# A projection in three fp32r products: high and low parts made by ScalarE and GpSimd

## The chip, the cores and the metric

The kernel runs on one core of a Trainium2 chip. The metric is device time in microseconds of one execution; three timed runs of the kernel before gave 1002.29, 999.23 and 1001.32 us, median 1001.32. TensorE (PE) multiplies matrices, VectorE (DVE), ScalarE (ACT) and GpSimd (POOL) do elementwise work, SyncE (SP) issues most transfers. Each engine works through its own list in order and waits on semaphores.

## The reference

One block of a graph network on 3125 nodes with 256 features and 50000 edges: a graph attention layer, a mixing layer in hyperbolic space and a layer of eight experts, each added to the rows. The change concerns the first product of the graph attention alone:

```python
xn = _layernorm(x, axis=-1)
h_prime = (xn @ W + b).reshape(n, 8, 32)
h_src = jnp.sum(h_prime * a_src, axis=2)      # per node and head
h_trg = jnp.sum(h_prime * a_trg, axis=2)
```

The attention weights per edge come from h_src[src] + h_trg[trg] through leaky_relu and exp, and the rows h_prime[src] are summed per target with these weights. The later parts use h_prime only through these sums.

## The kernel before

**Tiles.** The 3125 nodes are 25 tiles of 128 (NT = 25). The features are two chunks of 128 (KC = 2). `FM` (traced as feat_rows) holds x transposed, features on partitions; it is loaded from a transposed copy of x in three parts of 8, 8 and 9 tiles (ROW_PARTS, semaphores xt_part). `x_in` holds x with nodes on partitions, in the same three parts, for the row statistics.

**Weights.** TensorE turns the centred W into bank `b_hte` (line 822) and multiplies it with the attention vectors into `b_z` (lines 827 and 829). ScalarE copies both into `wx`, 256 + 16 = 272 columns (HW) for each chunk, and the bias row into `hbias` (lines 538 to 541, semaphore wx_ready, 3 in the end).

**Projection.** `project(t)` on TensorE (line 839) multiplies tile t of FM, as the stationary operand, with `wx` in plain f32, two matmuls of 272 columns in the program (four records in the trace, bank<-oh,feat_rows, line 847), into one of eight banks (AHEAD = 8): it waits until the bank's tile eight before has been read (hst_done). VectorE's `project(t)` (line 1265) scales the first 264 columns with the row's inverse deviation, adds the bias row and writes ACC (traced as sums; semaphore hp_ready). ScalarE's `targets_part(t)` (line 547) waits for hp_ready, takes the last 16 columns into `hst` (line 549) and signals hst_done. SP stores each row tile of ACC to the table projected_rows (line 403).

**Order around it.** VectorE's list: statistics of part 0 (`part_stats`, lines 1212 to 1221), `part_roots(0)`, then the 25 tiles, with part_stats(1) and (2) after tiles 3 and 10 and part_roots(1) and (2) after tiles 5 and 12; then the norms of the rows (from line 1231). ScalarE's list: `inverse_root` for part 0, then targets_part for the 25 tiles, with inverse_root for parts 1 and 2 after tiles 3 and 10 (lines 553 and 554); each waits for the statistics of that part. TensorE warms up with transposes (line 815) before. GpSimd makes constants, waits for the target numbers, casts them to 16 bits (`d16`, line 508), and then starts the edge gathers (line 503), which wait for all 25 stores of projected rows. SP sends d16 out before the store of tile TARGETS_IN (20).

**Behind the projection** TensorE turns the normalised rows (line 836) and forms their covariance (line 879), 33 groups of edges are gathered, weighted and summed (lines 1389, 1443, 923), beside the mixing layer; then the experts follow in two layers and an output, which are already done as three fp32r products of high and low parts (lines 1051 to 1053).

Of the kernel before, what the change touches and what calls it, by code (L numbers as in the profile page):

```python
# [9 lines left out]
F32 = mybir.dt.float32  # L10
# [46 lines left out]
CUT = 18  # L57
LEAD = 2
AHEAD = 8
ROW_PARTS = [(0, 8), (8, 16), (16, NT)]  # L60
TURNED = 8
WARM = 24
# [1 line left out]
LEADING = 2  # L64
STATS_AT = {3: 1, 10: 2}
ROOTS_AT = {5: 1, 12: 2}
TARGETS_IN = 20
PARTS = 3
XS = 4

# [67 lines left out]
def program(nc, a, out):  # L138
    with ExitStack() as ctx:
# [48 lines left out]
            x_all = early_sb("x_in", NT * XP)  # L188
        x_in = x_all[:, :].rearrange("p (t f) -> p t f", f=XP)


        FM = sb("feat_rows", [P, KC, NPAD])
        mixed = FM[:, :, :].rearrange("p c (t n) -> p t c n", n=P)
# [87 lines left out]
        xst = [uflat[:, i * XS * F:(i + 1) * XS * F].rearrange("p (t f) -> p t f", f=F) for i in range(2)]  # L281
        d16 = ohT[1][:, :].bitcast(I16)[0:NG, 0:EG]
        ohf = [oh[i][:, :, :].rearrange("p c w -> p (c w)") for i in range(2)]
        wx = ohf[0][:, 0:KC * HW].rearrange("p (k n) -> p k n", k=KC)
        hbias = ohf[0][:, KC * HW:(KC + 1) * HW]
        wT = ohf[1][:, 0:KC * F].rearrange("p (c n) -> p c n", c=KC)
        bcolb = ohf[1][:, KC * F:KC * F + 256].rearrange("p (c m) -> p c m", c=KC)
# [15 lines left out]
        for names_ in (  # L303
            "x_pad x_last xt_pad wa_in w_in b_in w_mix w_ffn edge_fill edges idn ablk_zero consts",
            "vchain achain gchain rsq_in rsq_out",
            "wt_ready wt_mm wa_ready wa_mm wx_ready hst_done rng_ready rng_mm dst_in d16_ready d16_out",
            "rows_in xs_ready sym_tr tr_done fs_ready proj_mm hp_ready tout",
            "cm_in cm_tr cm_red cm_mm exs_in exs_out k_mm shifted cov_mm s_copied",
            "sw_mm prod_ready var_mm baff_ready acc_init",
            "z_mm z_evac u_mm u_evac fsq_ready qk_ready eps_ready",  # L310
            "o_ready o_tr oT_ready r_mm mixed_ready no2_ready",
            "dstb_free win_tmp win_ready hte_ready z_part z_done zl_ready exp_done msg_ready",
            "seg_ready acc_done g_free xoT xhte xoh xseg",
            "ft_ready nf2_ready th_in th_out m_ready faff_in faff_out wr_hi wr_lo",
            "mx_tr mx_red mx_mm winv_ready weighed rstd_in rstd_out xs2_in xs2_ready tr2_done",
            "frh_ready frl_ready lg_mm sm_in sm_out gates g3_hi g3_in gt_tr gt_ready bo_clear bo_in bo_mm x2b ff_ready scaled rows_added",
            "w_hi w_lo h1_mm h1_r h1_hi h1_lo h2_mm h2_r h2_hi h2_lo y_mm y_add y_tile out_done out_act",
        ):
            s.update({k: sem(k) for k in names_.split()})
# [152 lines left out]
        @block.gpsimd  # L472
        def _(pool):
            g = nc.gpsimd
            chain = Chain(pool, s["gchain"])
            g.memset(x_in[:, NT - 1, 0:F], 0.0).then_inc(s["x_pad"], 1)
            g.memset(FM[:, :, N:NPAD], 0.0).then_inc(s["xt_pad"], 1)
            g.memset(ablk[:, :, :], 0.0).then_inc(s["ablk_zero"], 1)
            g.memset(ones[:, :], 1.0).then_inc(s["consts"], 1)
            chain.link(g.memset(ident[:, :], 0.0))  # L480
            g.affine_select(out=ident[:, :], in_=ident[:, :], compare_op=ALU.not_equal, fill=1.0, base=0,
                            pattern=[[-1, P]], channel_multiplier=1).then_inc(s["idn"], 1)
            g.memset(src_l[:, NG - 1, :], 0).then_inc(s["edge_fill"], 1)
            g.memset(dst_l[:, NG - 1, :], PAD_DST).then_inc(s["edge_fill"], 1)
            g.memset(ip[:, 1:MC + 1, :], 0.0).then_inc(s["consts"], 1)
            g.iota(row_i, pattern=[[1, P]], base=0, channel_multiplier=0).then_inc(s["consts"], 1)
            g.iota(col_i[:, :], pattern=[[0, 1]], base=0, channel_multiplier=1).then_inc(s["consts"], 1)
            g.memset(avg[:, :], 1.0 / P).then_inc(s["consts"], 1)
            g.memset(x_in[:, :, F:XP], 1.0).then_inc(s["consts"], 1)

            def gather(grp):
                slot, t, paced, settled = grp % SLOTS, grp - LEAD - MIX0, grp >= SLOTS, grp >= 2 * SLOTS
                need(pool, s["g_free"], grp - SLOTS + 1)
                if paced:
                    need(pool, s["msg_ready"], grp - LEAD)
                elif grp == 3:
                    pool.wait_ge(s["cov_mm"], 1)
                for c in range(CHUNKS[grp]):
                    if settled and c == 5:
                        need(pool, s["hte_ready"], grp - LEAD + 2)  # L500
                    if settled and c == 9 and t < NT:
                        pool.wait_ge(s["u_mm"], 3 * t + 3)
                    g.indirect_dma_start(  # L503
                        out=G[slot][:, c, :], out_offset=None, in_=table[:, :],
                        in_offset=bass.IndirectOffsetOnAxis(ap=src_l[:, grp, c:c + 1], axis=0),
                    ).then_inc(gath[slot], 16)
            pool.wait_ge(s["dst_in"], 48)
            g.tensor_copy(d16, dst_rows).then_inc(s["d16_ready"], 1)
            pool.wait_ge(s["edges"], 16 * 6)
            pool.wait_ge(s["tout"], 16 * NT)  # L510
            for grp in range(NG):
                gather(grp)

            pool.wait_ge(s["r_mm"], NT)
            g.memset(bo_raw, 0.0).then_inc(s["bo_clear"], 1)
# [3 lines left out]
        def _(act):  # L519
# [15 lines left out]
                    ins = A.copy(ablk[rows, c, h:h + H + 1:H], acol[rows, c:c + 3:2])  # L535
            ins.then_inc(s["wa_ready"], 1)
            act.wait_ge(s["wt_mm"], 1)
            A.copy(wx[:, :, 0:F], b_hte[:, :].rearrange("p (k f) -> p k f", k=KC)).then_inc(s["wx_ready"], 1)
            act.wait_ge(s["wa_mm"], 1)
            A.copy(wx[:, :, F:HW], b_z[:, 0:KC * 2 * H].rearrange("p (k h) -> p k h", k=KC)).then_inc(s["wx_ready"], 1)  # L540
            A.copy(hbias[:, F:HW], b_z[:, 64:64 + 2 * H]).then_inc(s["wx_ready"], 1)

            def turned(t):
# [13 lines left out]
                A.activation(x_in[:, t, 0:F], x_in[:, t, 0:F], ACT.Identity, bias=nd["nb"][:, t:t + 1], scale=nd["scale"][:, t:t + 1]).then_inc(s["xs_ready"], 1)  # L557

            inverse_root(nd["rstd"], nd["t1"], 1, slice(*ROW_PARTS[0]))
            for t in range(NT):  # L560
                targets_part(t)
                if t in STATS_AT:
                    inverse_root(nd["rstd"], nd["t1"], STATS_AT[t] + 1, slice(*ROW_PARTS[STATS_AT[t]]))
# [246 lines left out]
        def _(pe):  # L810
# [26 lines left out]
                ins.then_inc(s["tr_done"], 1)  # L837

            def project(t):
                for i, (lo, hi) in enumerate(ROW_PARTS):  # L840
                    if t == lo:
                        pe.wait_ge(xt_part[i], 16)
                if t == NT - 1:
                    pe.wait_ge(s["xt_pad"], 1)
                need(pe, s["hst_done"], t - AHEAD + 1)
                for c in range(KC):
                    ins = T.matmul(project_bank(t)[:, 0:HW], FM[:, c, t * P:(t + 1) * P], wx[:, c, :], start=(c == 0), stop=(c == KC - 1))  # L847
                ins.then_inc(s["proj_mm"], 1)

            keep_busy(WARM_TOO)  # L850
            pe.wait_ge(s["wx_ready"], 3)
            for t in range(NT):
                project(t)

# [316 lines left out]
        def _(dve):  # L1171
# [109 lines left out]
                                rng_f[:, :, None].broadcast_to([NG, 4, NG]), ALU.mult).then_inc(s["rng_ready"], 1)  # L1281

            part_stats(0)
            part_roots(0)
            dve.wait_ge(s["wx_ready"], 3)
            dve.wait_ge(s["b_in"], 16)
# [598 lines left out]
```

## Time and profile before

| | |
|---|---|
| timed runs | 1002.29, 999.23, 1001.32 us |
| profiled execution | 999.06 us, span 997.0 us |
| busy, share of the span | PE 907.3 us (91%), DVE 751.3 (75%), ACT 582.0 (58%), POOL 378.2 (38%) |
| projection on TensorE | 12.10 to 36.14 us, 100 recorded matmuls |
| its accumulations on VectorE | 14.27 to 36.67 us, 25 |
| first edge gather | 39.76 us |

Times in the trace count from the span's start. A busy share is an average over all stages; the stage of the change is the first 40 us, and what it is bound by is read from the rows below. The chain of waits goes back from the last instruction to what released it. PEclk is the granted clock of TensorE, 1.00 being 2.4 GHz and 0.50 being 1.2 GHz.

### The profile page before, as it was taken

To read this page: it belongs to the slowest core of one execution; us is meant where nothing else is said; L and a number is where in the kernel's file an instruction comes from. 1 tells how busy PE (TensorE), PEld (TensorE's weight loads), DVE (VectorE), ACT (ScalarE), POOL (GpSimd) and SP (SyncE) were. 2 spreads that over 40 slices of the span, in tenths; PEclk is the share of its full clock that TensorE was granted. 3 is DMA by queue.
4 is the path that set the end of the run, shared out by engine and by line. 5 is a ranking of instruction groups with operands and counts; after the bars stand their busy time and mean duration, and the time that the engine had idled before them with its cause. 6 is when DMAs were issued, how large, how long until landed. Compare 5 with 4: busy or idle time off the path is not lost.

```text
span 997.0 us, 14575 instructions
## 1 busy us (share of the span) xinstructions
PE 907.3 (91%) x4968; PEld 786.9 (79%) x4968; DVE 751.3 (75%) x1465; ACT 582.0 (58%) x1210; POOL 378.2 (38%) x410
## 2 busy tenths in 40 slices
PE   8698799999989988887654899999999999999997
PEld 7487688888877877776543788998989888888886
DVE  6978788887767668777787788876565777777877
ACT  2370366666655666565144657767566666676764
POOL 1377777777777777777772000000000000000000
PEclk9888899999999999999777899999999999999999
DMA  9844545445545545545663012001010000000013
GB/s 309 265 107 134 146 140 140 133 134 141 142 125 139 140 125 141 142 126 140 175 183 93 1 33 77 1 1 33 1 33 1 27 6 15 19 1 1 1 42 87
DMA packets 51176, 92.18 MB, mean 92 GB/s; under 512 B 9780, under 2 KB 33384, under 8 KB 51083
## 3 DMA queue, kind: packets, MB, share of 16 engines
q0 software_dynamic: 18768, 52.88, 19.7%
q1 hardware_dynamic: 31596, 37.86, 12.1%
q8 instruction: 50, 0.82, 0.3%
q10 hardware_dynamic: 719, 0.27, 0.1%
q14 instruction: 43, 0.35, 0.1%
HBM read 84.30 MB, written 6.68 MB: 91 GB/s over the span
## 4 chain that ended last, share of the span: by engine, by line
PE 50%; POOL 23%; issue 10%; DVE 10%; ACT 5%; DMA 1%; DVEq 0%; POOLq 0%; ACTq 0%
POOL G L503 23%; PE bank L1051 9%; PE bank L1053 9%; PE bank L1052 9%; PE bank L923 4%; PE bank L1117 3%; PE bank L1120 3%; PE bank L847 2%; PE bank L958 2%; PE bank L879 2%; PE bank L1118 1%; PE bank L1119 1%; PE bank L969 1%; ACT hid L748 1%; DVE G L1443 1%
## 5 line engine op out<-in xcount | busy, mean ns | idle before, releaser
L503 POOL DMA_INDIRECT G<-projected_rows,src_l x391 | 373.8, 956 | 131.7 <-issue 117.3
L748 ACT ACTIVATE hid<-bank,faff 128x512 f32<-128x512 f32 (+2 forms) x224 | 157.1, 722 | 104.1 <-PE bank L1053 102.2
L923 PE MATMUL bank<-G,oh 128*128 128x264 f32 x782 | 188.3, 399 | 20.3 <-DVE G L1443 20.1
L923 PEld LDWEIGHTS bank<-G,oh 128*128 128x128 f32 x782 | 153.4, 197 | 48.6 <-DVE G L1443 21.3
L1443 DVE TENSOR_TENSOR G<-G,bank 128x3072 f32<-128x3072 f32 (+1 forms) x33 | 109.1, 3306 | 0.0
L958 PE MATMUL bank<-feat_rows,wqkv 128*128 128x256 f32 (+1 forms) x312 | 77.5, 395 | 19.2 <-ACT TT L624 8.1
L1741 DVE TENSOR_TENSOR hil<-hid,hil 128x1024 fp32r<-128x1024 f32 (+2 forms) x56 | 60.8, 1085 | 40.6 <-ACT hil L758 40.4
L958 PEld LDWEIGHTS bank<-feat_rows,wqkv 128*128 128x128 f32 x312 | 60.6, 202 | 30.7 <-ACT TT L624 10.2
L1051 PE MATMUL bank<-frh,ew 128*128 128x512 f32 (+3 forms) x228 | 84.0, 368 | 0.8 <-ACT hid L748 0.7
L1053 PE MATMUL bank<-frh,ew 128*128 128x512 f32 (+3 forms) x228 | 82.4, 362 | 0.0
L1052 PE MATMUL bank<-frl,ew 128*128 128x512 f32 (+3 forms) x228 | 82.4, 361 | 0.0
L1051 PE MATMUL bank<-hil,ew 128*128 128x512 f32 (+2 forms) x224 | 81.6, 364 | 0.0
L1053 PE MATMUL bank<-hil,ew 128*128 128x512 f32 (+2 forms) x224 | 81.2, 362 | 0.0
L1052 PE MATMUL bank<-hil,ew 128*128 128x512 f32 (+2 forms) x224 | 81.1, 362 | 0.0
L587 ACT ACTIVATE G<-zed,negc 128x96 f32<-128x96 f32 (+1 forms) x33 | 12.5, 379 | 98.7 <-DVE zed L1416 98.7
L1389 DVE TENSOR_REDUCE zed<-bank 128x96 f32<-128x288 f32 (+1 forms) x33 | 14.9, 451 | 61.5 <-DMA G<-projected_rows,src_l 57.8
L1761 DVE SCALAR_TENSOR_TENSOR feat_rows<-bank,gate,feat_rows 128x256 f32<-128x256 f32 (+1 forms) x117 | 56.6, 484 | 4.1
L1420 DVE TENSOR_TENSOR oh<-key,bank 128x1536 f32<-128x1536 f32 (+1 forms) x33 | 56.9, 1724 | 2.0 <-ACT bank L591 2.0
L1760 DVE SCALAR_TENSOR_TENSOR feat_rows<-bank,gate,feat_rows 128x256 f32<-128x256 f32 (+1 forms) x117 | 55.6, 475 | 0.0
L758 ACT CAST hil<-hid 128x1024 fp32r<-128x1024 f32 (+2 forms) x56 | 52.7, 942 | 4.4
L1741 DVE TENSOR_TENSOR even<-hid,even 128x1024 fp32r<-128x1024 f32 (+2 forms) x28 | 30.5, 1089 | 32.3 <-ACT even L758 32.3
L1741 DVE TENSOR_TENSOR odd<-hid,odd 128x1024 fp32r<-128x1024 f32 (+2 forms) x28 | 30.4, 1087 | 26.9 <-ACT odd L758 26.9
(345 smaller groups left out, 2021.6 us busy)
## 6 DMA issues: line engine op xcount, KB each, us to landing
dstb<-targets SPq DMA_DIRECT2D x32, 384.0 KB, 3.8
G<-projected_rows,src_l POOLq DMA_INDIRECT x391
projected_rows<-sums SPq DMA_DIRECT2D x25, 132.0 KB, 2.2
x_in<-in_x SPq DMA_DIRECT2D x3, 1024.0 KB, 11.5
out<-feat_rows SPq DMA_DIRECT2D x23, 128.0 KB, 2.2
feat_rows<-in_xT SPq DMA_DIRECT2D x2, 1024.0 KB, 11.3
U<-in_x SPq DMA_DIRECT2D x4, 512.0 KB, 6.6
TT<-in_W SPq DMA_DIRECT2D x8, 256.0 KB, 3.2
```

The source lines that it names most:

```text
L503: g.indirect_dma_start(out=G[slot][:, c, :], out_offset=None, in_=table[:, :], in_offset=bass.IndirectOffsetOnAxis(ap=src_l[:, grp, c:c + ...
L748: A.activation(hid[layer][:, m, 0:cols], bank[2 * layer + m][:, 0:cols], ACT.Relu, bias=faff[:, 2 * layer + 1, j:j + 1], scale=faff[:, 2 * ...
L923: ins = T.matmul(b_seg[g % 2][:, 0:ROW], oh[g % 2][:, c, :], G[g % SLOTS][:, c, :], start=(c == 0), stop=(c == ch - 1))
L958: ins = T.matmul(b_z[:, i * 256:i * 256 + cols], wqkv[:, k, c * P:(c + 1) * P], FM[:, k, start:start + cols], start=(k == 0), stop=(k == K ...
L1051: T.matmul(out_, lh, rh, start=(k == 0), stop=False)
L1052: T.matmul(out_, lh, rl, start=False, stop=False)
L1053: return T.matmul(out_, ll, rh, start=False, stop=(k == KC - 1))
L1420: return V.tensor_tensor(out_, keys[:, :, None].broadcast_to([P, ch, P]), b_seg[par][:, ROWC:ROWC + P][:, None, :].broadcast_to([P, ch, P] ...
L1443: V.tensor_tensor(m3, m3, exps(par, ch)[:, :, :, None].broadcast_to([P, ch, H, DH]), ALU.mult).then_inc(s["msg_ready"], 1)
L1741: V.tensor_tensor(hidl[layer][par][:, :, 0:cols], hid[layer][:, :, 0:cols], hidh[layer][par][:, :, 0:cols].bitcast(F32), ALU.subtract).the ...
L1760: link(V.scalar_tensor_tensor(out=m, in0=high, scalar=gate[0:rows, t, e:e + 1], in1=m, op0=ALU.mult, op1=ALU.add))
L1761: ins = V.scalar_tensor_tensor(out=m, in0=low_, scalar=gate[0:rows, t, e:e + 1], in1=m, op0=ALU.mult, op1=ALU.add)
```

## The change

The product x W is split in three: with x = xh + xl and W = Wh + Wl, where xh and Wh are the values rounded to fp32r, it adds xh Wh, xh Wl and xl Wh, for both chunks, so six fp32r matmuls of 272 columns per tile. ScalarE rounds the tiles of FM into a ring of 12 tiles (`xh`), eight ahead of targets_part in its list, tile 0 still before the weights are complete and tiles 1 to 7 after inverse_root of part 0. GpSimd subtracts (`xl = FM - xh`) into a second ring, tile after tile, and casts the targets after tile 21 (TARGETS_IN is 22 now). VectorE makes the low part of the weights in two subtractions, between part_stats(0) and part_roots(0). TensorE waits for wx_low, and per tile for xh and xl in place of the loads. The rings lie where the edge gathers' buffers G0 to G2 are later. Left out below are the line of semaphore names and the removed `wx`.

```diff
+RING = 12
+SPLIT_AHEAD = 8
-TARGETS_IN = 20
+TARGETS_IN = 22
...
+            x_split = [ring_sb(f"x_split{i}", RING * F) for i in range(2)]
+            w_split = [ring_sb(f"w_split{i}", KC * HW) for i in range(2)]
...
-            pool.wait_ge(s["dst_in"], 48)
-            g.tensor_copy(d16, dst_rows).then_inc(s["d16_ready"], 1)
+            pool.wait_ge(s["xt_pad"], 1)
+            for t in range(NT):
+                pool.wait_ge(s["xh_ready"], t + 1)
+                need(pool, s["proj_mm"], t - RING + 1)
+                g.tensor_tensor(xl[:, t % RING], FM[:, :, t * P:(t + 1) * P], xh[:, t % RING].bitcast(F32), ALU.subtract).then_inc(s["xl_ready"], 1)
+                if t == TARGETS_IN - 1:
+                    pool.wait_ge(s["dst_in"], 48)
+                    g.tensor_copy(d16, dst_rows).then_inc(s["d16_ready"], 1)
...
+            def high_rows(t):
+                for i, (lo, hi) in enumerate(ROW_PARTS):
+                    if t == lo:
+                        act.wait_ge(xt_part[i], 16)
+                if t == NT - 1:
+                    act.wait_ge(s["xt_pad"], 1)
+                need(act, s["proj_mm"], t - RING + 1)
+                A.copy(xh[:, t % RING], FM[:, :, t * P:(t + 1) * P]).then_inc(s["xh_ready"], 1)
+
+            high_rows(0)
             act.wait_ge(s["wa_mm"], 1)
...
             inverse_root(nd["rstd"], nd["t1"], 1, slice(*ROW_PARTS[0]))
+            for t in range(1, SPLIT_AHEAD):
+                high_rows(t)
             for t in range(NT):
+                if t + SPLIT_AHEAD < NT:
+                    high_rows(t + SPLIT_AHEAD)
                 targets_part(t)
...
             def project(t):
-                for i, (lo, hi) in enumerate(ROW_PARTS):
-                    if t == lo:
-                        pe.wait_ge(xt_part[i], 16)
-                if t == NT - 1:
-                    pe.wait_ge(s["xt_pad"], 1)
+                pe.wait_ge(s["xh_ready"], t + 1)
+                pe.wait_ge(s["xl_ready"], t + 1)
                 need(pe, s["hst_done"], t - AHEAD + 1)
+                o = project_bank(t)[:, 0:HW]
                 for c in range(KC):
-                    ins = T.matmul(project_bank(t)[:, 0:HW], FM[:, c, t * P:(t + 1) * P], wx[:, c, :], start=(c == 0), stop=(c == KC - 1))
+                    T.matmul(o, xh[:, t % RING, c], wxh[:, c, :], start=(c == 0), stop=False)
+                    T.matmul(o, xh[:, t % RING, c], wxl[:, c, :], start=False, stop=False)
+                    ins = T.matmul(o, xl[:, t % RING, c], wxh[:, c, :], start=False, stop=(c == KC - 1))
                 ins.then_inc(s["proj_mm"], 1)
 
             keep_busy(WARM_TOO)
             pe.wait_ge(s["wx_ready"], 3)
+            pe.wait_ge(s["wx_low"], 2)
...
             part_stats(0)
+            dve.wait_ge(s["wx_ready"], 1)
+            V.tensor_tensor(wxl[:, :, 0:F], b_hte[:, :].rearrange("p (k f) -> p k f", k=KC), wxh[:, :, 0:F].bitcast(F32), ALU.subtract).then_inc(s["wx_low"], 1)
+            dve.wait_ge(s["wx_ready"], 3)
+            V.tensor_tensor(wxl[:, :, F:HW], b_z[:, 0:KC * 2 * H].rearrange("p (k h) -> p k h", k=KC), wxh[:, :, F:HW].bitcast(F32), ALU.subtract).then_inc(s["wx_low"], 1)
             part_roots(0)
```

## Rows read from the trace of the kernel before

**Rows 1.** Chain of waits, 10 to 50 us: start, us, what.
```profile
12.31 23.85 PE bank L847 x100
```

**Rows 2.** Waits, 0 to 48 us: total us, times, longest.
```profile
POOL G L503 <- DMA projected_rows<-sums: 12.9, 1, 12.9
...
DVE sums L1267 <- PE bank L847: 2.0, 5, 0.4
```

**Rows 3.** Timeline of VectorE, 12 to 38 us: start, us, instruction, [idle before].
```profile
12.66 0.17 DVE L1221 TENSOR_SCALAR nodes<-mv 128x8 f32<-128x8 f32 x1
...
15.10 0.49 DVE L1267 SCALAR_TENSOR_TENSOR sums<-bank,nodes,oh 128x264 f32<-128x264 f32 x1 [0.33 <-PE bank L847]
...
16.93 0.49 DVE L1267 SCALAR_TENSOR_TENSOR sums<-bank,nodes,oh 128x264 f32<-128x264 f32 x1 [0.42 <-PE bank L847]
...
24.98 3.02 DVE L1210 BATCH_NORM_STATS2 stats<-x_in 128x6 f32<-128x256 f32 x9
...
28.98 0.17 DVE L1221 TENSOR_SCALAR nodes<-mv 128x9 f32<-128x9 f32 x1
...
30.67 4.17 DVE L1267 SCALAR_TENSOR_TENSOR sums<-bank,nodes,oh 128x264 f32<-128x264 f32 x10
35.26 0.49 DVE L1267 SCALAR_TENSOR_TENSOR sums<-bank,nodes,oh 128x264 f32<-128x264 f32 x1 [0.42 <-PE bank L847]
36.18 0.49 DVE L1267 SCALAR_TENSOR_TENSOR sums<-bank,nodes,oh 128x264 f32<-128x264 f32 x1 [0.42 <-PE bank L847]
```

**Rows 4.** Timeline of TensorE in the expert layers, 699 to 712 us.
```profile
701.66 0.28 PE L1051 MATMUL bank<-ew,odd 128*128 128x256 f32 x1
...
704.41 0.28 PE L1053 MATMUL bank<-ew,odd 128*128 128x256 f32 x1
...
705.33 0.34 PE L1052 MATMUL bank<-frl,ew 128*128 128x384 f32 x1
...
707.06 0.33 PE L1053 MATMUL bank<-frh,ew 128*128 128x384 f32 x1
```

**Rows 5.** Timeline of TensorE, 7 to 12.5 us: the second warm-up block.
```profile
10.26 2.05 PE L815 MATMUL bank<-ip 128*128 128x128 f32 x10
```

**Rows 6.** Stretches: us, busy of PE, PEld, DVE, ACT, POOL, PEclk, DMA share, GB/s.
```profile
10.50:11.00 0.50, 0.50 (x5) 0.50 (x4) 0.50 (x3) 0.21 (x2) 0.00 (x0) 0.62 1.09 387
...
14.00:14.50 0.50, 0.50 (x4) 0.42 (x3) 0.36 (x2) 0.00 (x0) 0.00 (x0) 0.97 1.03 410
...
41.00:41.50 0.50, 0.00 (x0) 0.00 (x0) 0.43 (x3) 0.00 (x0) 0.30 (x1) 0.84 1.06 399
...
58.00:58.50 0.50, 0.50 (x4) 0.45 (x3) 0.50 (x3) 0.19 (x1) 0.50 (x1) 0.59 0.88 211
```

**Rows 7.** VectorE's instructions by line and shape: count, busy us, mean ns, idle before.
```profile
L1716 DVE TENSOR_TENSOR frl<-bank,frh 128x512 fp32r<-128x512 f32 x11 | 7.5, 691 | 6.8 <-ACT frh L730 6.8
```

**Rows 8.** Instructions that write feat_rows, 0 to 48 us: the loads, issue to landing.
```profile
L383 SPq DMA_DIRECT2D feat_rows<-in_xT x3: 592/3485/3692, 1.7 to 11.5; - x3
...
DMA to landing us min/median/max: 9.1/13.0/13.6
```

**Rows 9.** ScalarE's instructions by line and shape.
```profile
L635 ACT ACTIVATE exr<-feat_rows 128x256 bf16<-128x256 f32 x25 | 10.4, 416 | 6.8 <-DVE feat_rows L1567 5.3
...
L549 ACT ACTIVATE hst<-bank,nodes 128x16 f32<-128x16 f32 x25 | 6.8, 273 | 8.7 <-DVE sums L1267 7.0
...
L730 ACT CAST frh<-bank 128x256 fp32r<-128x256 f32 x3 | 1.1, 376 | 0.0
```

**Rows 10.** Timeline of ScalarE, 29 to 37.5 us: inverse_root of the third part.
```profile
29.19 0.21 ACT L553 ACTIVATE nodes<-nodes 128x9 f32<-128x9 f32 x1 [3.82 <-DVE nodes L1221]
```

**Rows 11.** GpSimd's instructions by line and shape.
```profile
L503 POOL DMA_INDIRECT G<-projected_rows,src_l x391 | 373.8, 956 | 131.7 <-issue 117.3 <-DMA projected_rows<-sums 12.9 <-DVE G L1443 0.6
L508 POOL CAST ohT<-U 33x1536 int16<-33x1536 int32 x1 | 1.5, 1456 | 22.0 <-DMA U<-in_dst 22.0
...
L476 POOL MEMSET x_in<- 128x256 f32 x1 | 0.3, 311 | 0.3 <-POOLq L1878 0.3
```

More of the change, by code:

```diff
@@ L189, in program, with ring_sb @@
         x_in = x_all[:, :].rearrange("p (t f) -> p t f", f=XP)
+        with ExitStack() as ring_stack:
+            def ring_sb(name, columns_, dt=F32R):
+                return ring_stack.enter_context(nc.sbuf_tensor(name, [P, columns_], dt))
+            ring_sb("ring_under_rows", KC * NPAD, F32)
+            ring_sb("ring_under_sums", (NT + 1) * ROW, F32)
+            x_split = [ring_sb(f"x_split{i}", RING * F) for i in range(2)]
+            w_split = [ring_sb(f"w_split{i}", KC * HW) for i in range(2)]
+        xh, xl = (b[:, :].rearrange("p (t k n) -> p t k n", t=RING, k=KC) for b in x_split)
+        wxh, wxl = (b[:, :].rearrange("p (k n) -> p k n", k=KC) for b in w_split)
         FM = sb("feat_rows", [P, KC, NPAD])
@@ L283, in program @@
         ohf = [oh[i][:, :, :].rearrange("p c w -> p (c w)") for i in range(2)]
-        wx = ohf[0][:, 0:KC * HW].rearrange("p (k n) -> p k n", k=KC)
         hbias = ohf[0][:, KC * HW:(KC + 1) * HW]
@@ L305, in program @@
             "vchain achain gchain rsq_in rsq_out",
-            "wt_ready wt_mm wa_ready wa_mm wx_ready hst_done rng_ready rng_mm dst_in d16_ready d16_out",
+            "wt_ready wt_mm wa_ready wa_mm wx_ready wx_low xh_ready xl_ready hst_done rng_ready rng_mm dst_in d16_ready d16_out",
             "rows_in xs_ready sym_tr tr_done fs_ready proj_mm hp_ready tout",
@@ L537, in _ @@
             act.wait_ge(s["wt_mm"], 1)
-            A.copy(wx[:, :, 0:F], b_hte[:, :].rearrange("p (k f) -> p k f", k=KC)).then_inc(s["wx_ready"], 1)
+            A.copy(wxh[:, :, 0:F], b_hte[:, :].rearrange("p (k f) -> p k f", k=KC)).then_inc(s["wx_ready"], 1)
+            def high_rows(t):
[7 more added lines that the diff above has]
+            high_rows(0)
             act.wait_ge(s["wa_mm"], 1)
-            A.copy(wx[:, :, F:HW], b_z[:, 0:KC * 2 * H].rearrange("p (k h) -> p k h", k=KC)).then_inc(s["wx_ready"], 1)
+            A.copy(wxh[:, :, F:HW], b_z[:, 0:KC * 2 * H].rearrange("p (k h) -> p k h", k=KC)).then_inc(s["wx_ready"], 1)
             A.copy(hbias[:, F:HW], b_z[:, 64:64 + 2 * H]).then_inc(s["wx_ready"], 1)
```

## The prediction

> **What bounds the kernel now.** I read the chain of waits first. It runs straight through the projection: 23.85 us of matmuls of line 847 from 12.31 us on [rows 1], then VectorE's last accumulation of line 1267, then the small node arithmetic and the turning of the rows. So what counts is when the last accumulation ends: 36.18 + 0.49 = 36.67 us [rows 3]. The second thing that starts there is GpSimd's gather, which waits until all 25 tiles of projected rows are stored [rows 2]; it moves with the same end. I therefore carry a shift of this end one to one to the end of the kernel.
>
> The chain names TensorE, but the wait view corrects it: in the whole projection VectorE waits for line 847 only 2.0 us, in five pieces [rows 2]. The order of VectorE's work shows why [rows 3]. It waits a little in tiles 1 to 3, falls behind while it takes the second and the third part of the row statistics (3.02 us of BATCH_NORM_STATS2 for the third, plus small steps), and then catches up: ten accumulations in 4.17 us, 0.42 us each, back to back from 30.67 us. Only tiles 23 and 24 wait for TensorE again, 0.42 us each. So TensorE and VectorE are level at the end, and a faster TensorE alone can win no more than about those two waits, and only if nothing else comes late.
>
> **TensorE's own work.** Before: four recorded matmuls of a tile; the last two accumulations start 0.92 us apart [rows 3], so about 0.23 us per pass. After: six single-precision-round (fp32r) matmuls with 272 columns. The expert layers have such products: 24 with 256 columns start 701.66 to 704.41, that is 0.120 us each, and 11 with 384 columns start 705.33 to 707.06, 0.173 us each [rows 4]. For 272 columns I interpolate 0.127 us, so 0.76 us per tile, 19.0 us for 25 tiles against some 23: about 4 us less TensorE work, if its clock is high.
>
> **The start.** TensorE's warm-up ends at 12.31 [rows 5], and the first product followed at once. Now it waits for wx_low, the low part of the weights. VectorE makes that after part_stats(0), which signals at about 12.8 (12.66 + 0.17, [rows 3]), in two subtractions. The nearest row of the large one (PSUM minus SBUF into fp32r, 128x512) is 691 ns [rows 7]; the small one (32 columns) is bounded by the 0.17 us of the tiny steps. End: about 13.7. ScalarE meanwhile waits for the first third of the transposed rows, which is there no sooner than 1.7 + 9.1 = 10.8 us [rows 8], and rounds tile 0; GpSimd's subtraction of tile 0 ends about 12; neither is late. So TensorE starts at 13.75, not at 12.1, and is idle for some 1.4 us.
>
> That gap touches the clock. The granted clock fell to half (1.2 GHz) at about 10.6 and was full again (2.4 GHz) from 14.0 [rows 6], with TensorE busy without a gap from the second warm-up block on [rows 5]. With a gap in that stretch I don't expect the return at 14.0. At 1.2 GHz a tile costs 6 x 272 / 1.2 GHz = 1.36 us. Only the first four tiles count here, because VectorE waits for TensorE only up to tile 3. If the clock is high at once, tile 3 is streamed at 13.75 + 4 x 0.76 = 16.8; if all four run low, at 19.2. I take 18.4, nearer to the low clock, because after the next long gap the clock stayed low from 41.4 to 58.4, long after TensorE had work again [rows 6]. VectorE starts about 0.25 us behind a tile's stream (before, tile 1 was streamed at 14.85, two tiles from 12.1 at 0.92 per tile and twice that before 14.0, and accumulated from 15.10), so its accumulation of tile 3 starts at 18.65, where it was 16.93 [rows 3]: 1.7 us late; by the two ends 0.1 or 2.5 us late.
>
> From there to tile 22 VectorE's list is the same and nearly without waits, and TensorE is ahead of it, so the 1.7 us are carried: the third part's statistics signal at 30.85 (before about 29.15, 28.98 + 0.17) and the burst may begin at 32.4.
>
> **The end.** Here the new queues decide. ScalarE has 25 more copies of 128x256 from SBUF. The nearest rows are 376 ns (cast from PSUM) and 416 ns (square from SBUF) [rows 9]; I take 0.41, with 0.27 for the head column (line 549) 0.65 us per tile as they overlap a little. Spread over 23 us this hides behind VectorE. But high_rows(19) stands behind inverse_root(2) in ScalarE's order, and that waits for the third part's statistics: before, 29.19 [rows 10], now about 30.9, done 31.35. So tiles 19 to 24 are rounded at 31.8, 32.4, 33.05, 33.7, 34.3, 35.0, and TensorE, which could have finished tile 18 by about 30, waits for them. VectorE is covered by the finished banks for that time.
>
> GpSimd's 25 subtractions are not in the trace (two inputs, 128x256). From below: a memset of 256 columns, 311 ns. From above: the longest GpSimd row, 956 ns. Between: the cast with one input took 1456 ns for 1536 elements, 0.95 ns each [rows 11]; with 0.1 us fixed, one reading of 256 is 0.34 and two readings 0.59. I take 0.65 with its two waits. The GPSIMD Engine Reference of the Trainium skill (section 3.1) gives 4497 ns for a two-input add of 2048 fp32 elements; an estimate from that page is 0.6 us for 256, and the sum would stay as it is; no run so far shows it.
>
> Tiles 19 to 21 leave GpSimd at 32.45, 33.1, 33.75. Then the cast of the targets, 1.46 us [rows 11], stands in the same queue, at tile 21: it was hidden at 25.4 before, now it stands before tiles 22 to 24, and no product of theirs may start without it. They come at 35.85, 36.5, 37.15. TensorE needs 0.76 us each: tile 24 is streamed at 38.2, VectorE accumulates it from 38.4 to 38.9. Against 36.67 that is **2.2 us later**. Without the cast in the way it would be 37.8; with VectorE alone as the bound 37.4. The cast's result itself (SP's store at tile 22) delays nothing, as the stores of tiles 22 to 24 come later anyway.
>
> **Sum.** The profiled execution took 999.06 us (span 997.0, 2.1 around it). 999.06 + 2.2 = 1001.3. The three timed runs have the median 1001.32, and the mean of all four is 1000.5, so the profiled one was a quick one; I put the forecast at 1000.5 + 2.2 = **1002.7**. The 4 us of TensorE work buy nothing, since VectorE was level with it.
>
> **Rivals.**
> Rival A, VectorE alone bounds: the clock returns as early as before, and the rounding and the subtraction of the last tiles arrive in time, so that the waits of tiles 23 and 24 (0.84 us) and 0.4 us of their TensorE tail vanish: 1.2 us faster, 999.3. For it: VectorE's 0.42 us per tile is a firm row. Against it: the order behind inverse_root(2) and the cast at tile 21.
> Rival B, GpSimd becomes the bound. It decides from 0.76 us per subtraction on, TensorE's own pace. At 0.956, its upper bound, tile t leaves it at about 13.8 + 0.96 t: tile 21 at 34.9 with tile 22 queued, the cast to 36.4, tile 24 at 39.3, accumulated at 40.8: 4.1 us slower, 1004.6. For it: 25 two-input operations that no row shows. The SBUF page of the Trainium skill ("Who interferes with whom") says that a VectorE instruction with two SBUF inputs and a GpSimd instruction that reads SBUF shut each other out; VectorE's long operations here have at most one, so I give that no time of its own.
> Rival C, a second drop of the clock: TensorE waits up to 2.5 us at tile 19, and the last six tiles run at 1.36 instead of 0.76 us, 3.6 us more: 5.8 us slower, 1006.3. Against it: TensorE did almost nothing from 36.1 on, and the clock fell only at 41.4 [rows 6].
> Rival D, the products don't run at the rate of the expert layers (272 columns lie between measured 256 and 384, so I doubt it); at 0.23 us each a tile costs 1.38 us, and 25 of them last from 13.75 to 48.3, 12 us longer than before: 1012.5.
>
> **Chances.** Forecast (0 to 3 us slower) 0.62; A 0.15; B 0.13; C 0.07; D 0.03. What a measurement of this kernel can tell from no change is 0.3%, 3.0 us. Faster by more would need a gain that VectorE's list has no room for, 0.06; slower by more is B, C, D and the upper part of the forecast, 0.24; the same 0.70. The range runs from A to C, 999.2 to 1006.3; the forecast's own is 1000.5 to 1003.8.
>
> **What would show it.** The first product at about 13.7 and the clock still low at 14.0 and back before 19; products 0.127 us apart; VectorE's accumulation of tile 3 at 18.6; ScalarE's copies at 0.41, GpSimd's subtractions near 0.6 to 0.65 us; TensorE waiting for the subtraction at tile 19 and at tile 22 behind the cast; the last accumulation ending at about 38.9. The prediction is wrong if that end lies before 36.5, or if the end shifts and the total doesn't follow it.

## The result, and the profile after

The changed kernel took 1004.12 us in the median of six runs (1002.91 to 1004.54) against 999.22 us for six runs of the kernel before (998.47 to 1002.29): a ratio of 1.0037 with a 95% interval of [1.0027, 1.0047], which is 3.7 us slower. (The two medians lie 4.9 us apart, since the six runs of before scatter over 3.8 us.) The profiled execution took 1004.07 us with a span of 1002.2 us, 5.0 us more than the profiled one of before. The forecast was 2.2 us slower. The direction and most of the steps came as written, and one step on the path failed: VectorE's list did not stay as long as it was.

Waits of the changed kernel, 0 to 48 us (total us, times, longest), to hold against [rows 2]:

```profile
POOL x_split L522 <- ACT x_split L564: 16.1, 5, 8.0
...
DVE sums L1300 <- PE bank L879: 2.0, 5, 0.8
...
PE bank L877 <- POOL x_split L522: 2.6, 1, 2.6
...
PE bank L877 <- DVE w_split L1320: 1.8, 1, 1.8
```

TensorE has two new waits, one for the low weights and one for GpSimd's subtraction. VectorE waits for TensorE 2.0 us in five pieces, as much as before, so its own list still fills the rest of the stage, and that list has grown. Its timeline in the changed kernel, to hold against [rows 3] (L1300 is the accumulation, L1243 the row statistics, L1209 to L1212 the four small Newton steps of `part_roots`):

```profile
11.46 0.70 DVE L1218 TENSOR_TENSOR mv<-stats 128x8 f32<-128x8 f32 x1
12.09 0.16 DVE L1219 TENSOR_TENSOR mv<-stats 128x8 f32<-128x8 f32 x1
...
18.53 0.49 DVE L1300 SCALAR_TENSOR_TENSOR sums<-bank,nodes,oh 128x264 f32<-128x264 f32 x1 [0.26 <-PE bank L879]
18.94 2.70 DVE L1243 BATCH_NORM_STATS2 stats<-x_in 128x6 f32<-128x256 f32 x8
...
23.48 0.15 DVE L1209 TENSOR_TENSOR nodes<-nodes 128x8 f32<-128x8 f32 x1
23.67 0.72 DVE L1210 TENSOR_TENSOR nodes<-nodes 128x8 f32<-128x8 f32 x1
24.42 0.66 DVE L1211 TENSOR_SCALAR nodes<-nodes 128x8 f32<-128x8 f32 x1
25.11 0.67 DVE L1212 TENSOR_TENSOR nodes<-nodes 128x8 f32<-128x8 f32 x1
25.82 2.09 DVE L1300 SCALAR_TENSOR_TENSOR sums<-bank,nodes,oh 128x264 f32<-128x264 f32 x5
27.82 3.03 DVE L1243 BATCH_NORM_STATS2 stats<-x_in 128x6 f32<-128x256 f32 x9
...
32.71 0.16 DVE L1209 TENSOR_TENSOR nodes<-nodes 128x9 f32<-128x9 f32 x1
32.90 0.70 DVE L1210 TENSOR_TENSOR nodes<-nodes 128x9 f32<-128x9 f32 x1
33.64 0.66 DVE L1211 TENSOR_SCALAR nodes<-nodes 128x9 f32<-128x9 f32 x1
34.34 0.65 DVE L1212 TENSOR_TENSOR nodes<-nodes 128x9 f32<-128x9 f32 x1
35.02 4.72 DVE L1300 SCALAR_TENSOR_TENSOR sums<-bank,nodes,oh 128x264 f32<-128x264 f32 x11
40.00 0.49 DVE L1300 SCALAR_TENSOR_TENSOR sums<-bank,nodes,oh 128x264 f32<-128x264 f32 x1 [0.25 <-PE bank L879]
```

The same steps in the kernel before (L1176 to L1179 there), on the same timeline of VectorE:

```profile
21.89 0.16 DVE L1176 TENSOR_TENSOR nodes<-nodes 128x8 f32<-128x8 f32 x1
...
22.97 2.09 DVE L1267 SCALAR_TENSOR_TENSOR sums<-bank,nodes,oh 128x264 f32<-128x264 f32 x5 [0.31 <-DVE nodes L1179]
...
29.86 0.16 DVE L1176 TENSOR_TENSOR nodes<-nodes 128x9 f32<-128x9 f32 x1
30.05 0.17 DVE L1177 TENSOR_TENSOR nodes<-nodes 128x9 f32<-128x9 f32 x1
30.26 0.17 DVE L1178 TENSOR_SCALAR nodes<-nodes 128x9 f32<-128x9 f32 x1
30.47 0.17 DVE L1179 TENSOR_TENSOR nodes<-nodes 128x9 f32<-128x9 f32 x1
```

Steps over eight or nine columns that took 0.17 us take 0.65 to 0.72 us. The third part's group of four lasts from 32.71 to 35.02, 2.31 us, where it lasted from 29.86 to 30.67, 0.81 us. The second part's lasts 2.34 us (23.48 to 25.82); in the trace before it ran from 21.89 to 22.97, 1.08 us, 0.31 of it a wait. GpSimd's timeline in the changed kernel says what else goes on at those times:

```profile
11.40 0.73 POOL L522 TENSOR_TENSOR x_split<-feat_rows,x_split 128x256 fp32r<-128x256 f32 x1 [8.05 <-ACT x_split L564]
13.86 7.67 POOL L522 TENSOR_TENSOR x_split<-feat_rows,x_split 128x256 fp32r<-128x256 f32 x11 [1.73 <-ACT x_split L564]
23.63 2.13 POOL L522 TENSOR_TENSOR x_split<-feat_rows,x_split 128x256 fp32r<-128x256 f32 x3 [2.09 <-ACT x_split L564]
26.99 2.83 POOL L522 TENSOR_TENSOR x_split<-feat_rows,x_split 128x256 fp32r<-128x256 f32 x4 [1.23 <-ACT x_split L564]
32.86 2.10 POOL L522 TENSOR_TENSOR x_split<-feat_rows,x_split 128x256 fp32r<-128x256 f32 x3 [3.04 <-ACT x_split L564]
34.91 1.45 POOL L525 CAST ohT<-U 33x1536 int16<-33x1536 int32 x1
```

Every long small step lies inside a run of subtractions (11.46 in the first, 23.67 to 25.11 in the third, 32.90 to 34.34 in the fifth; two Newton steps of the first part, at 14.01 and 14.66, took 0.62 and 0.65 us in the second), and every short one outside, or begun just before a run starts (23.48, 32.71) or as it ends (12.09). The long Newton steps of the second and third part start 0.75, 0.69 and 0.74, 0.70 us apart, which is the pace of the subtractions (7.67 us for eleven, 0.70 each): here VectorE gets one small step in for each subtraction. L1210 and L1212 read two tensors in SBUF; L1211, a TENSOR_SCALAR, reads only one and is as long (0.66), so two inputs are not the whole condition.

The order of the kernel makes them meet. ScalarE's `inverse_root` releases two things at once: the Newton steps on VectorE, and, because the roundings queue behind it, the next three roundings and with them three subtractions.

The end of the projection is then a sum of four pieces. The accumulation of tile 3 starts 1.6 us later (18.53 against 16.93 [rows 3]); the second group costs 2.34 - 1.08 = 1.26 us more and the third 2.31 - 0.81 = 1.50; and the two waits for TensorE at the end (0.84 us [rows 3]) have become one of 0.25; short waits inside the merged rows and rounding make up the 0.05 that is left. That is +3.8: the last accumulation ends at 40.49 instead of 36.67.

Stretches of the changed kernel (columns as in [rows 6]; PEclk is third from the end):

```profile
16.00:17.00 1.00, 1.00 (x6) 1.00 (x6) 0.24 (x2) 0.59 (x3) 1.00 (x2) 0.50 1.09 351
17.00:18.00 1.00, 1.00 (x10) 1.00 (x9) 0.61 (x2) 0.85 (x3) 1.00 (x2) 0.99 1.10 352
30.00:33.00 3.00, 1.07 (x9) 0.84 (x7) 2.83 (x15) 0.94 (x5) 0.14 (x1) 1.00 0.02 7
33.00:34.00 1.00, 0.32 (x2) 0.35 (x3) 0.96 (x2) 0.71 (x3) 1.00 (x2) 1.00 0.64 221
34.00:35.00 1.00, 1.00 (x7) 1.00 (x6) 0.95 (x2) 0.00 (x0) 1.00 (x3) 0.54 0.14 50
35.00:37.00 2.00, 2.00 (x11) 2.00 (x10) 1.98 (x5) 1.45 (x7) 2.00 (x2) 0.50 0.25 87
```

The clock is low (0.50, 1.2 GHz) until 17.0 and comes back with TensorE busy. It falls a second time at 34.0, after TensorE had stood for 2.62 us, until 33.69, behind `inverse_root(2)`. There VectorE is mostly the later of the two: it is busy 1.98 of the 2.00 us from 35 to 37.

### The profile page after: what moved, and what is told of

It is laid out like the page before. It is cut to its first block, busy times and chain, and to the rows that moved or that the text cites. A ratio compares the mean times of both kernels' runs of the same rounds, so it can differ in the third digit from the quotient of the medians.

```text
span 1002.2 us, 14765 instructions
## 1 busy us (share of the span) xinstructions
PE 906.0 (90%) x5018; PEld 788.9 (79%) x5018; DVE 756.2 (75%) x1467; ACT 588.2 (59%) x1235; POOL 395.9 (40%) x435
## 4 chain that ended last, share of the span: by engine, by line
PE 47%; POOL 27%; issue 11%; DVE 9%; ACT 4%; DMA 1%; POOLq 0%; DVEq 0%; ACTq 0%
POOL G L514 26%; PE bank L1084 10%; PE bank L1086 9%; PE bank L1085 9%; PE bank L956 3%; PE bank L1150 2%; PE bank L1153 2%; PE bank L912 2%; PE bank L991 2%; PE bank L1151 1%; PE bank L1152 1%; POOL x_split L522 1%; ACT hid L780 1%; PE bank L1002 1%; PE bank L868 1%
```

## The experiments

The theory was that VectorE's small steps wait for GpSimd's subtractions (the lock theory). The rivals were that the late start after the low weights, or the clock that is low in it, makes the loss; that TensorE, starved at tile 19, does; and that the total follows something after the projection. The runs were made in three jobs, each on one chip with its own runs of the kernel before: e1, e2, e3, e5 beside a median of 1001.64 us (23 runs, 998.93 to 1004.48), e4, e6, e7, e8 beside 999.86 us (27), c1, c2 beside 1000.58 us (20). The kernel before thus moves by 1.8 us between the jobs, so totals of different jobs are compared by their ratios, and the totals expected in microseconds only loosely. "End" is the end of the last accumulation.

**e1: no subtraction.** The third product takes the high rows again, so the term of low rows times high weights is left out of the result; the cast of the targets runs first on GpSimd.

```diff
-                g.tensor_tensor(xl[:, t % RING], ..., ALU.subtract).then_inc(s["xl_ready"], 1)
...
-                pe.wait_ge(s["xl_ready"], t + 1)
...
-                    ins = T.matmul(o, xl[:, t % RING, c], wxh[:, c, :], ...)
+                    ins = T.matmul(o, xh[:, t % RING, c], wxh[:, c, :], ...)
```

> The changed kernel without GpSimd's subtraction: the third product of each tile takes the high part xh in place of xl (so xl Wh is left out of the result), TensorE has as many matmuls as before, and GpSimd casts the targets as early as in the kernel before. Theory (lock): GpSimd's subtractions shut out VectorE's small two-input Newton steps in part_roots(1) and (2), 2.3 us each instead of 0.8 to 1.1. Without them the steps are back at 0.17 us and the last accumulation ends at 40.49 - 1.25 - 1.5 = 37.7 us, give or take 0.4; total about 1001.3. Rival (starved TensorE): the loss is made by TensorE's wait of 2.6 us behind inverse_root(2) and the second drop of its clock, and the Newton steps are only long in passing; this order on ScalarE is left as it is, so the last accumulation stays at 39.5 us or later and the total at 1003 or more.

Median 1001.35 us, ratio 0.9994 [0.9983, 1.0006]. All Newton steps are back at 0.16 to 0.17 us, although ScalarE still rounds beside them, so its roundings are not what makes them long. The end, 38.98, lies between the two theories, 1.3 us later than mine: tile 3 came 0.6 us later than in the changed kernel (19.12), and without the long steps VectorE arrives earlier and now meets TensorE, whose clock was at 0.50 from 33 to 36 us after a similar pause (four waits of 0.20 to 0.41 us). The total equals the median of before in this job, but not because the end does, which is 2.3 us later than 36.67: the profiled execution, 1001.20, is 2.1 us above the profiled one of before (999.06). That the total came out as expected is in part luck.

**e2: the kernel before, with 29 idle subtractions.** GpSimd subtracts rows into a buffer that nobody reads yet; besides, the cast of the targets stands among the subtractions, and two later waits make sure that they are done.

```diff
+            for t in range(29):
+                rows = FM[:, :, t % 8 * P:(t % 8 + 1) * P]
+                g.tensor_tensor(G[t // EC][:, t % EC, 0:F]..., rows, rows, ALU.subtract).then_inc(s["extra"], 1)
...
```

> The kernel before with 29 subtractions of 128x256 on GpSimd alone, from the landing of the first third of the transposed rows on, back to back until about 33 us, their results unused; nothing else of the change. Theory (lock): the small steps of VectorE with two inputs from SBUF take up to 0.7 us each in the statistics and in the Newton steps, wherever a subtraction runs; the last accumulation ends 2 to 7 us later than 36.67 and the total rises by as much, to 1001 to 1006; the matmuls stay as they are. Rival (starved TensorE): TensorE's list and ScalarE's are those of before, so the end stays within 0.5 us of 36.67 and the total within 1 us of 999.2.

Median 1007.99 us (1003.74 to 1010.8), ratio 1.0066 [1.0042, 1.0089]. VectorE's timeline, with the Newton steps of the first and of the second part:

```profile
15.43 0.62 DVE L1183 TENSOR_TENSOR nodes<-nodes 128x8 f32<-128x8 f32 x1 [0.52 <-ACT nodes L560]
16.08 0.54 DVE L1184 TENSOR_TENSOR nodes<-nodes 128x8 f32<-128x8 f32 x1
...
19.40 2.70 DVE L1217 BATCH_NORM_STATS2 stats<-x_in 128x6 f32<-128x256 f32 x8
...
24.95 0.16 DVE L1183 TENSOR_TENSOR nodes<-nodes 128x8 f32<-128x8 f32 x1
25.14 0.17 DVE L1184 TENSOR_TENSOR nodes<-nodes 128x8 f32<-128x8 f32 x1
```

GpSimd's timeline of the same run:

```profile
10.82 12.62 POOL L510 TENSOR_TENSOR G<-feat_rows 128x256 f32<-128x256 f32 x22 [7.47 <-DMA feat_rows<-in_xT]
...
27.02 4.03 POOL L510 TENSOR_TENSOR G<-feat_rows 128x256 f32<-128x256 f32 x7
```

With no other part of the change, the same steps are long inside the run of subtractions and short after it (of fifteen small steps that began in that run, three slipped through at 0.16 to 0.19 us). The statistics proper are not slowed: eight in 2.70 us inside the run, 0.34 each, like the nine in 3.02 of [rows 3]. Nor are the accumulations. So it is the small steps and GpSimd's subtraction, whatever TensorE computes. The end was 39.4, 2.7 us late, as expected. The total was not: the runs spread over 7 us, their median lies above the 1006 that I had allowed, and the profiled execution (1003.74) is the fastest of the six. Where the rest of this kernel's loss arises stays open.

**e3: low weights earlier**, inside the statistics of the first part.

```diff
+                    if t == 3:
+                        dve.wait_ge(s["wx_ready"], 1)
+                        V.tensor_tensor(wxl[:, :, 0:F], ..., ALU.subtract).then_inc(s["wx_low"], 1)
...
```

> The changed kernel with VectorE's two subtractions for the low weights moved into the first part's statistics (the large one after four of the eight BATCH_NORM_STATS2, the small one after the eighth). Theory (the start costs 1.6 us by TensorE's gap and the clock that stays low): the first product follows the warm-up at about 12.2, the clock is back at about 14, VectorE's accumulation of tile 3 starts at 16.3 to 17.0 instead of 18.53, and the end comes 1.5 to 2 us earlier, total about 1002.3. Rival (the loss comes only from the lock and the end, and the start is made up by VectorE's slack later): the end stays within 0.4 us of 40.49 and the total at 1004.

Median 1004.54 us, ratio 1.0025 [1.0013, 1.0038]. The first product came at 12.23 and the clock stayed high (1.00 from 12 to 19 us), yet tile 3 was accumulated only at 17.43: tile 1 now waited for its subtraction (GpSimd's second run still begins at 14.03). Of the 1.1 us gained there only 0.4 are left at the end (40.11): the statistics' small steps moved into that GpSimd run and took 0.48 and 0.78 us. This is what the rival had said (an end within 0.4 us of 40.49): an earlier start is worth little while the lock moves along. That the edit kept the clock high is not shown: in other executions it fell at other times (at 10.2 in the changed kernel, 12.4 in e1).

**e4: seven more warm-up transposes.**

```diff
-WARM_TOO = 10
+WARM_TOO = 17
```

> The changed kernel with 17 in place of 10 transposes in the second warm-up block, so that TensorE has work until the low weights are there and its clock comes back earlier. Theory (lock): the accumulation of tile 3 comes about 1 to 1.5 us earlier, but then the statistics of part 1 end while GpSimd's first run of subtractions still goes on (it ended at 21.5 us), their small steps get long in turn, and the end of the projection gains 0.5 us at most: total 1003.5 to 1004.2. Rival (the start's 1.6 us are lost for good by the clock and come back with it): the end is 1 us or more earlier, total 1003 or less.

Median 1003.77 us, ratio 1.0033 [1.002, 1.0046]. TensorE had no pause, but at 0.50 the 17 transposes lasted from 10.86 to 14.73, so the first product came at 14.37 instead of 13.80, and the clock returned only between 16 and 17 us (0.82). Tile 3 came at 18.55, so nothing was gained, where both theories had expected at least 1 us. The clock was already at 0.50 from 10 us on in this execution. Since the start did not move, the run does not test what it was made for, and what the gap and the low clock cost at the start stays untested.

**e5: eleven tiles ahead instead of eight.**

```diff
-SPLIT_AHEAD = 8
+SPLIT_AHEAD = 11
```

> The changed kernel with ScalarE rounding eleven tiles ahead in place of eight (SPLIT_AHEAD 11), so that TensorE has rounded tiles up to 21 before inverse_root(2). Theory (lock): TensorE's wait of 2.6 us and the second drop of the clock go away, but they are covered by VectorE's catching up; as long as a subtraction runs beside part_roots the end moves by no more than 0.5 us, total 1003.5 to 1004.2; if the subtractions move out of part_roots the Newton steps get short and the end comes up to 2.7 us earlier, and the two go together. Rival (starved TensorE): the end comes 2 us or more earlier although the Newton steps stay long.

Median 1006.65 us, ratio 1.0047 [1.0032, 1.0061], slower still. The longer GpSimd run (fourteen subtractions, 13.99 to 23.76) now covers the second part's statistics. VectorE's timeline has the longest small step of all runs:

```profile
22.10 1.70 DVE L1217 TENSOR_TENSOR nodes<-stats 128x8 f32<-128x8 f32 x1
```

It began inside that run and ended with it (23.80), after more than two subtractions. TensorE's clock fell again (0.50 from 35 to 38 us), but the last twelve accumulations ran without a wait for it and ended at 42.08, so starvation of TensorE is not what sets the end here. The lock theory had allowed 0.5 us, and missed: I had not looked where the longer run would end.

**e6: Newton operands in PSUM**, for the second and third part; everything is computed.

```diff
+        def moved(v, i):
+            at = 0 if v is nd["t1"] else 64
+            return bank[7][:, at:at + NT] if i else v
...
-AHEAD = 8
+AHEAD = 7
...
```

> The changed kernel with the variance and the temporary of the Newton steps of parts 1 and 2 in a PSUM bank kept free for it (seven banks for the projection in place of eight), so that none of the four steps has two inputs from SBUF; GpSimd's subtractions stay where they are. Theory (lock, through VectorE's second way into SBUF): the four steps take 0.2 us each although subtractions run beside them, part_roots(1) and (2) last 0.8 to 1.0 us in place of 2.3; the end moves forward by 1.2 to 1.6 us only, because TensorE, late behind inverse_root(2) and at the low clock, is the next bound; total about 1002.5. Rival (VectorE is slowed by anything GpSimd does, not by the port): the steps stay at 0.6 us or more and the total does not fall.

Median 1002.06 us, ratio 1.002 [1.0011, 1.0029]; end 38.87, 1.6 us sooner. GpSimd's timeline of this run:

```profile
13.94 7.68 POOL L527 TENSOR_TENSOR x_split<-feat_rows,x_split 128x256 fp32r<-128x256 f32 x11 [1.82 <-ACT x_split L569]
...
31.10 2.13 POOL L527 TENSOR_TENSOR x_split<-feat_rows,x_split 128x256 fp32r<-128x256 f32 x3 [2.77 <-ACT x_split L569]
```

VectorE's timeline, with the last two Newton steps of the first part, whose operands stay in SBUF, and the four of the third:

```profile
14.08 0.61 DVE L1267 TENSOR_SCALAR nodes<-nodes 128x8 f32<-128x8 f32 x1
14.73 0.65 DVE L1268 TENSOR_TENSOR nodes<-nodes 128x8 f32<-128x8 f32 x1
...
30.98 0.16 DVE L1265 TENSOR_TENSOR bank<-nodes,bank 128x9 f32<-128x9 f32 x1
31.18 0.18 DVE L1266 TENSOR_TENSOR bank<-bank,nodes 128x9 f32<-128x9 f32 x1
31.39 0.17 DVE L1267 TENSOR_SCALAR bank<-bank 128x9 f32<-128x9 f32 x1
31.59 0.17 DVE L1268 TENSOR_TENSOR nodes<-nodes,bank 128x9 f32<-128x9 f32 x1
```

The same lines (L1267, L1268) take 0.61 and 0.65 us beside subtractions with their operands in SBUF, and 0.17 us beside subtractions with the variance and the temporary in PSUM: the multiplications then read one operand in SBUF, the TENSOR_SCALAR none. (The first multiplications come in another order, and the projection has seven banks.) That is the lock, switched off by the place of the operands. The two groups last 0.81 and 0.82 us, 3.0 us less than in the changed kernel, and tile 3 came 0.7 us sooner (17.85); of these 3.7 us, 1.6 reach the end: TensorE, at 0.50 from 33 to 35 us, is now what VectorE waits for (0.81 us and three times 0.26), and a step of the second part's statistics, at 21.00, took 0.65 us beside a subtraction.

**e7: e1, and tiles 19 to 21 rounded before `inverse_root(2)`** (the same term is left out).

```diff
...
+                if t == 10:
+                    for tt in range(19, 22):
+                        high_rows(tt)
...
```

> As e1 (no subtraction on GpSimd, third product with xh in place of xl), and in addition ScalarE rounds tiles 19 to 21 ahead of inverse_root(2), so that TensorE is not left without work before the last tiles. In e1 the last four accumulations waited 1.1 us for TensorE, whose clock had dropped. Theory (lock first, starved TensorE second): these waits go, the end comes 0.7 to 1.1 us earlier than in e1 (38.98), total 1000.3 to 1001. Rival (TensorE's wait costs nothing, VectorE's list alone sets the end): no change against e1, within 0.3 us.

Median 1000.57 us, ratio 1.0005 [0.9996, 1.0014]. The clock stays at 1.00 from 29 to 39 us, the last twelve accumulations run without a wait, and the end is 36.39. VectorE's timeline:

```profile
31.50 4.89 DVE L1296 SCALAR_TENSOR_TENSOR sums<-bank,nodes,oh 128x264 f32<-128x264 f32 x12
```

That is 2.6 us before e1's end, more than expected, partly because tile 3 was 1.1 us earlier than in e1 here. So without lock and starvation the end is where it was before (36.67), and VectorE's list bounds. The faster products do buy something: these twelve took 6.00 us before (30.67 to 36.67), 1.1 us more, about the 1.2 us of rival A. But the later start takes as much away (tile 3 at 18.02, before 16.93).

**e8: the full product with all of it mended** (low weights early, tiles 1 to 3 and 18 to 20 rounded ahead of their `inverse_root`, Newton in PSUM, the cast after tile 14).

```diff
-SPLIT_AHEAD = 8
+SPLIT_AHEAD = 7
...
-TARGETS_IN = 22
+TARGETS_IN = 15
...
+                if t == 10:
+                    for tt in range(18, 21):
+                        high_rows(tt)
...
```

> The full product with what the runs point to: low weights made within the first statistics (as e3), tiles 1 to 3 rounded before inverse_root(0), rounding seven ahead, tiles 18 to 20 rounded before inverse_root(2), Newton steps of parts 1 and 2 through PSUM (as e6, seven banks), the cast of the targets after tile 14. Theory: tile 3 is accumulated by about 17, the Newton steps are short, only the small steps of the statistics can still meet a subtraction (0.5 to 1.5 us); the end at 36 to 37.3 and the total within 1 us of the kernel before. Rival (something else of the change costs, such as the banks or the transfers): the total stays above that of the kernel before by 2 us or more.

Median 1002.86 us, ratio 1.0023 [1.0014, 1.0033]; end 40.97, a miss by over 3 us. The total stays 3.0 us above before, as the rival had said, but not by banks or transfers. The Newton steps of the second and third part are short. The subtractions moved forward met the small steps that still lie in SBUF: those of the first part, two of its statistics (0.70 and 0.66 us) and two Newton steps (0.70 and 0.65), so that tile 3 came at 18.6 and not by 17, and those of the third part's statistics. VectorE's timeline there:

```profile
29.40 0.58 DVE L1227 TENSOR_TENSOR nodes<-stats 128x9 f32<-128x9 f32 x1
29.91 0.77 DVE L1228 TENSOR_TENSOR mv<-stats 128x9 f32<-128x9 f32 x1
30.60 0.76 DVE L1229 TENSOR_TENSOR mv<-stats 128x9 f32<-128x9 f32 x1
31.39 0.64 DVE L1230 TENSOR_TENSOR nodes<-nodes 128x9 f32<-128x9 f32 x1
```

GpSimd's run there lasts from 27.82 to 32.00. The delayed `inverse_root(2)` starved TensorE again, and the last five tiles waited for it.

**c1 and c2: the changed kernel unedited, and e6 again, on one chip.**

> The changed kernel unedited, beside the next one on one chip, so that the two can be compared in timed runs and not only in one profile each. If the shift in the projection is a steady one, the ratio to the kernel before lies again between 1.0027 and 1.0047 and the last accumulation ends within 0.4 us of 40.5. If it came from one lucky or unlucky phase of the clock, the ratio falls below 1.002.

> The kernel with the Newton operands of the second and third part in PSUM, on the same chip as the changed kernel. Lock theory: 1.2 to 2.2 us below the changed kernel's median, as the last accumulation ends 1.6 us sooner. Rival, that the end of the projection doesn't reach the total and only the clock's phase further on decides: within 0.7 us of the changed kernel.

c1: median 1004.08 us, ratio 1.0037 [1.0025, 1.0049], as in the first six runs. Its end was 41.29, outside my 0.4 us, because the clock came back only between 19 and 20 us there. It did not fall a second time in this execution (1.00 from 34 to 40 us), and the loss was the same, so that drop is not its cause. VectorE's last twelve accumulations:

```profile
36.15 5.14 DVE L1300 SCALAR_TENSOR_TENSOR sums<-bank,nodes,oh 128x264 f32<-128x264 f32 x12
```

c2: median 1001.40 us, ratio 1.0009 [0.9996, 1.0022]: 2.7 us below c1, above the 1.2 to 2.2 that I had allowed, with an end of 39.01. Part of the difference in the ends is c1's later clock (tile 3 at 19.65 against 18.51). Still, moving two small operands out of GpSimd's way takes back 2.7 of the 3.5 us that c1's median lies above before, in timed runs. No kernel here is faster than the one before beyond its interval.

## Why the prediction was right, and where its sum failed

- **First product at 13.75:** 13.80. **Clock still low at 14.0, tile 3 accumulated at 18.65:** back at 17.0, and 18.53. Right, but that tile 3 came within 0.12 us is in part luck: in c1, the same code, it came at 19.65, because the clock came back later.
- **Rates:** products 0.125 us apart at the high clock (0.127 predicted), ScalarE's copies 0.400 (0.41), GpSimd's subtractions 0.735 in the mean and 0.70 back to back (0.65).
- **"VectorE's list is the same and nearly without waits ... the 1.7 us are carried":** this is the step that failed. 1.6 us were carried to the second Newton group; there and in the third group the list grew by 2.76 us. In rival B the prediction had the rule beside it and gave it "no time of its own", because it looked at VectorE's long operations only. Most of the short ones have two inputs in SBUF; they lie on the path and run at the moment at which GpSimd is released. The third part's statistics signalled at 32.0 us, not at 30.85, and the burst began at 35.02, not at 32.4. Where the shared access was priced at nothing, it cost more than the whole forecast; e2 and e6 show it alone, on and off.
- **TensorE waits at tile 19:** 2.62 us measured, 2.5 in rival C. **The cast in front of tiles 22 to 24 costs 1.1 us** (38.9 against 37.8)**:** it ran at 34.91 as described and cost nothing that shows: the subtraction of tile 22 ended at about 37.05, and TensorE, busy without a pause, came to that tile only at 37.55. The forecast's end, 38.9, was thus built on the wrong queue. By its own figure for VectorE alone, 37.4, plus the 2.76, the end comes to 40.2; 40.49 was measured.
- **Luck in the number:** the 1.5 us that the wrong queue put on top of 37.4 stood in for more than half of the 2.76 us that were left out. Even so the 3.7 us lie outside the forecast's own 0 to 3 us, and the total, 1004.12, nearer to rival B's 1004.6 than to 1002.7, though GpSimd was not the bound as rival B has it. The range from A to C holds the total only because of rivals whose mechanisms are not what made the loss.
- **Rival C, a second drop of the clock:** it happened, at 34.0, and cost little, as VectorE was later. The twelve accumulations after the third group took 5.47 us (35.02 to 40.49), 5.14 in c1 with the clock high, and 4.89 in e5 and e7 without a wait: about 0.3 us for the drop, 0.6 us with the starvation. In e1 and e6, where VectorE is not later, TensorE is the bound at the end. The argument against it (the clock fell only at 41.4 after 36.1) did not hold here: TensorE had its pause of 2.62 us and was at work again for 0.3 us when the clock fell.
- **One to one to the end:** +3.8 us at the projection became +4.1 at the first gather (43.90 against 39.76) and +5.0 in the profiled execution, so the total followed. Over the twelve profiled executions the time from the end of the projection to the end of the execution lies between 962.2 and 964.4 us (before 962.4, changed 963.6, c1 962.6), so the end carries over to within about 2 us. Where the changed kernel's other 1.2 us arise stays open. Its clock differs further on (0.50 from 108 to 112 us, before 1.00), but c1 shows 0.52 there and has next to none of them.
- **Slips in its sums that changed nothing:** in rival B, tile 21 leaves GpSimd by 13.8 + 0.96 t at 33.96, not 34.9, which makes the rival 3.2 us slower, not 4.1; 0 to 3 us on 1000.5 is 1000.5 to 1003.5, not 1003.8; and 956 ns is not GpSimd's longest row, since the cast stands in the same rows with 1456 ns.

The Trainium skill's page "SBUF — State Buffer", section "Who interferes with whom", says that a VectorE instruction with two SBUF inputs and a GpSimd instruction that reads SBUF contend for a shared pair of ports, under an exclusive lock. The traces agree: 0.17 us becomes about 0.70, the length of one subtraction (in e5 once 1.70). It adds that `tensor_scalar`, with a single input, can enter a mode that takes the shared ports too. L1211 at 0.66 us fits, though no run here tells the mode.

## What to carry to other kernels

When work is given to GpSimd, list the VectorE instructions that run beside it by their operands, not by their length: a step of 0.17 us on operands in SBUF can cost as much as the GpSimd instruction it meets, and cost more once (1.70 us in e5). Look for one event that releases both, and put small operands that must run there into PSUM. And before an engine that is level with another is made faster, check what the other one's list will be; here some 4 us less of TensorE work, by the prediction's estimate, bought 1.1 us at the end (e7), and the later start took that back.

## What the runs showed of the hardware

- Beside back-to-back GpSimd subtractions of 128x256 (0.70 us each, 0.57 in e2), VectorE steps over 8 or 9 columns in SBUF mostly took 0.48 to 0.78 us instead of 0.16 to 0.17, once 1.70 (e5), with two SBUF inputs and as TENSOR_SCALAR with one; a few slipped through at 0.16 to 0.19 (e2). BATCH_NORM_STATS2 (0.34 us each) and accumulations out of PSUM (0.49) were not slowed.
- Newton steps with their variance and temporary in PSUM, so that the multiplications read one operand in SBUF and the TENSOR_SCALAR none, took 0.16 to 0.18 us beside the same subtractions (e6).
- The granted clock differs between executions: with the same code it came back to 2.4 GHz at 17.0 us in one and between 19 and 20 us in another (c1). In e4 TensorE had no pause from 10 us on and stayed at 1.2 GHz to past 16 us; in e3 it was at 2.4 GHz from 10 to 20 us, through pauses of 0.94 and 1.69 us.
